# Causal attention with routed experts on one core: the two heads of a pair on the two 64-row halves of TensorE for maxima and scores

## The chip, the cores and the metric

One core of a Trainium2 chip runs the program. The metric is the device time of one execution in microseconds (us); lower is better. Engines are called as in the profile: PE is TensorE's matmul, PEld its weight load, DVE is VectorE, ACT is ScalarE, POOL is GpSimd, SP is SyncE.

## The reference

A causal attention layer over one sequence of 2048 tokens of width 256, then a layer of 16 routed experts (two a token) and two shared ones, each with a residual and a layer norm. The change touches the attention alone:

```python
# x: (1, 2048, 256); 16 heads of 16; k and v come from a latent of 64
qf = jnp.concatenate([q_nope, q_rope], axis=-1)      # rotary on 12 of 16
kf = jnp.concatenate([k_nope, k_rope], axis=-1)
scores = jnp.einsum('bhqd,bhkd->bhqk', qf, kf) * scale
scores = jnp.where(causal, -jnp.inf, scores)
weights = jax.nn.softmax(scores, axis=-1)
out = jnp.einsum('bhqk,bhkd->bhqd', weights, v)
x = _layernorm(x + out)
x = _layernorm(x + experts(x))
```

## The kernel before, in words

**Work and its units.** The queries are cut into four chunks of 512 tokens (`CH`), the 16 heads into groups of four (`GH`). A unit is one group of one chunk: 16 units, four a chunk. A step is one unit and one block of 128 keys: a unit of chunk c has 4(c + 1) steps, in all 160. `aux_at`, `max_at` are lists that say what else each step does.

**Numbers of full precision from fast matmuls.** q and k are each split into a high and a low part in a reduced format (`F32R`), and the three products hi x hi, hi x lo, lo x hi (`PARTS`) are made in one matmul: the 16 dimensions of a head are stacked three times, 48 rows (`SPLIT`). `k_stack` holds two heads of a pair below one another, 96 rows (`STACK`), plus two rows of ones. `q_stack` holds for each head its 48 rows, with zeros in the rows of the pair's other head, plus two rows with the negated maxima in two parts. So one matmul of 96 rows makes one head's products, and one of 98 rows (`ROWS`) the same with the row's maximum taken off.

**Maxima first.** For each query and head the maximum over its keys is found before the scores. `max_bank` (line 637) fills one bank of PSUM, 128 queries by up to 512 keys, with four matmuls and a mask's matmul (line 642) for the four diagonal blocks of a head, with one or two matmuls for the rest of a head's own chunk (`SHARED_BANKS`: 128 + 384 keys, 256 keys), and with one of 512 keys for each earlier chunk. `max_ps` has three banks (`MAX_BANKS`); bank n waits on `max_done` until the reduction of bank n - 3 is done. DVE reduces each bank (`reduce_bank`, lines 761 and 767). `max_at` spreads the banks over the steps, 5.44, 4.48, 3.88 and 3.90 a step by chunk (`BANKS_A_STEP`), and has a unit's last bank at least three steps ahead of its first score (`MAX_AHEAD`). Units of chunk c have 12 + 16c banks. When a unit's banks are reduced, DVE folds them (line 778), the job `("maxima", u)` has PE transpose them (line 614), DVE negates and splits them into `m_rows` (lines 801, 802), and ACT issues two transfers of `m_rows` into the last two rows of `q_stack` (`store_maxima`, line 496).

**A step.** On PE (`score_head`, `values`, and the loop at the end of its block): four times a quarter of the step's banks and one score matmul, 128 keys by up to 512 queries (line 675; fewer queries on the diagonal, so that the last four steps of a unit have 512, 384, 256 and 128); auxiliary jobs after the second and the fourth; at the end the values of the step before, `values(s - 1)`, four heads with 17 output columns each at PSUM partitions 0, 32, 64, 96, in two passes each (line 695). Scores have three banks (`SCORE_BANKS`) and each waits on `exp_done` for the exponential three before it. In the last unit, where no maxima are left, the scores use the banks of both, six. ACT makes the exponentials (line 543), one a head, and its share of the auxiliary jobs after the second and fourth. POOL masks `probs` on the diagonal (line 450) and rotates and splits q and k of later chunks.

**Auxiliary jobs**: per chunk one latent, eight rotary and two value projections (`projection`), per unit the maxima's transpose and the output's (`out`), 62 of them after the prologue. The split q and k are stored to DRAM by SP and loaded back into `k_stack` and `q_stack` (`store_piece`, `load_q`, line 324).

**Prologue.** Chunk 0 is projected, the zeros of `q_stack` are set by POOL and DVE, the ones of `k_stack` by POOL, which copies them to the other chunks by DMA; unit 0's maxima are made and stored, then the first score runs.

The order of the work is that of the lists, the same on each engine; nothing is reordered at run time.

## Time and profile before

| | |
|---|---|
| time, median of 3 runs | 870.14 us (864.45 to 874.48) |
| the profiled execution | 869.14 us |
| its span | 867.4 us |
| PE busy | 758.3 us (87%) |
| PEld busy | 487.5 us (56%) |
| DVE busy | 571.0 us (66%) |
| ACT busy | 409.5 us (47%) |
| POOL busy | 243.7 us (28%) |
| line 637, maxima | 832 matmuls, 257.8 us |
| line 675, scores | 609 matmuls, 234.1 us (and 31 more into `max_ps`) |
| line 695, values | 1280 matmuls, 151.9 us, mean of one 547 ns |
| line 767 and 761, reductions | 640, 353.1 us |
| line 543, exponentials | 291.1 us; one of 512 columns 603 ns |
| line 496, copies of maxima | 32 transfers, 8.0 KB each, 1.9 us to landing |

Busy time of PE counts matmuls whose ends are modelled, and neighbours overlap in it; the distance between two starts says more. The attention ends at about 590 us of the span, the rest is the experts' half. The granted clock is a share of 2.4 GHz: 1.0 is 2.4 and 0.5 is 1.2 GHz.

### The profile page before, as it was taken

Reading aid. Unit: us, or ns where it says so; the run is one execution under the profiler, and the core shown is the slowest. Engines: PE = TensorE matmul, PEld = TensorE weight load, DVE = VectorE, ACT = ScalarE, POOL = GpSimd, SP = SyncE. Lnnn points to the kernel's source line nnn. Section 1 sums busy time; section 2 is a strip of 40 time slices with the busy share of each in tenths; the row PEclk is TensorE's granted clock in tenths of the full one; section 3 lists DMA queues with packets and bytes.
Section 4 is the critical chain, followed back from the end, with each engine's and each line's share of the span. In section 5 each row is a group of like instructions: output and inputs, shape, how many; then the busy total and the mean of one; then the engine's idle time right before and its main releaser. Section 6 shows DMA issues by size and latency. Waiting matters only on the chain. (4 is left out here: it accounts for less than half of the span.)

```text
span 867.4 us, 14346 instructions
## 1 busy us (share of the span) xinstructions
PE 758.3 (87%) x4309; PEld 487.5 (56%) x4310; DVE 571.0 (66%) x1414; ACT 409.5 (47%) x891; POOL 243.7 (28%) x327
## 2 busy tenths in 40 slices
PE   4679998999999999999999999992779999999930
PEld 3566565655645655566455555431569976666610
DVE  6755868778687877876778787202584456666646
ACT  3124464656555656666566666691412332222203
POOL 6326182341351043107100000102007513333323
PEclk9659999999999999999799999996798999999975
DMA  3754225140062006002400000003997313333245
GB/s 126 185 138 117 74 61 161 38 116 20 2 153 68 2 1 146 2 2 61 134 1 2 1 2 1 2 1 103 335 276 258 121 54 90 97 98 95 88 136 185
DMA packets 46668, 77.00 MB, mean 89 GB/s; under 512 B 5983, under 2 KB 27231, under 8 KB 45743
## 3 DMA queue, kind: packets, MB, share of 16 engines
q1 hardware_dynamic: 37455, 57.72, 24.9%
q0 software_dynamic: 5184, 14.72, 5.0%
q10 hardware_dynamic: 3968, 3.80, 1.3%
q8 instruction: 32, 0.52, 0.3%
q14 instruction: 29, 0.24, 0.1%
HBM read 42.40 MB, written 33.45 MB: 87 GB/s over the span
## 5 line engine op out<-in xcount | busy, mean ns | idle before, releaser
L543 ACT ACTIVATE probs<-scores 128x512 f32<-128x512 f32 (+3 forms) x609 | 291.1, 536 | 199.6 <-PE scores L675 182.2
L767 DVE TENSOR_REDUCE mx<-max_ps 128x1 f32<-128x512 f32 (+3 forms) x576 | 308.8, 594 | 79.3 <-PE max_ps L637 78.5
L637 PE MATMUL max_ps<-k_stack,q_stack 96*128 96x512 f32 (+3 forms) x832 | 257.8, 370 | 13.4 <-DVE mx L767 5.7
L675 PE MATMUL scores<-q_stack,k_stack 98*128 98x512 f32 (+3 forms) x609 | 234.1, 396 | 7.0 <-DMA q_stack<-m_rows 4.1
L637 PEld LDWEIGHTS max_ps<-k_stack,q_stack 96*128 96x128 f32 x832 | 150.8, 201 | 133.0 <-DVE mx L767 81.7
L695 PE MATMUL pv_ps<-probs,v_ones 128*17 128x512 f32 (+3 forms) x1280 | 151.9, 547 | 2.7 <-ACT probs L543 1.9
L675 PEld LDWEIGHTS scores<-q_stack,k_stack 98*128 98x128 f32 x609 | 117.7, 196 | 48.0 <-ACT probs L543 26.0
L450 POOL TENSOR_SCALAR_AFFINE_SELECT probs<-probs 128x512 f32<-128x512 f32 x64 | 40.6, 635 | 344.5 <-ACT probs L543 344.4
L1140 POOL DMA_INDIRECT token_y<-ys,dest x47 | 45.3, 964 | 100.0 <-DVE dest L1496 49.8
L761 DVE TENSOR_REDUCE mx<-max_ps 128x4 f32<-128x512 f32 x64 | 44.3, 692 | 35.5 <-PE max_ps L642 33.9
L1262 PE MATMUL gu_ps<-w_up_sb,xg_t 128*128 x188 | 67.3, 481 | 0.4 <-ACT xg_t L1199 0.3
L1179 ACT ACTIVATE silu<-gu_ps 128x176 f32<-128x176 f32 x79 | 24.9, 317 | 89.1 <-PE gu_ps L1262 44.9
L1442 DVE TENSOR_TENSOR hidden<-silu,gu_ps 128x176 f32<-128x176 f32 x79 | 26.6, 337 | 36.8 <-ACT silu L1179 35.7
L1290 PE MATMUL y_ps<-w_dn_sb,hidden_t 88*128 x188 | 48.5, 380 | 0.4 <-DVE ys L1502 0.4
L695 PEld LDWEIGHTS pv_ps<-probs,v_ones 128*17 128x17 f32 x1280 | 21.5, 96 | 46.9 <-ACT probs L543 35.1
L1130 POOL DMA_INDIRECT slot_x<-x_sb,slot x32 | 31.2, 974 | 47.5 <-DVE slot L1428 38.0
L1199 ACT ACTIVATE xg_t<-xt_ps 128x256 f32<-128x256 f32 x47 | 18.0, 383 | 49.8 <-PE xt_ps L1320 49.7
L1262 PEld LDWEIGHTS gu_ps<-w_up_sb,xg_t 128*128 128x128 f32 x188 | 31.9, 189 | 15.7 <-issue 2.2
L1489 DVE SCALAR_TENSOR_TENSOR part_w<-xg,expert_f 128x1 f32<-128x1 f32 x94 | 16.3, 215 | 36.1 <-DMA token_y<-ys,dest 35.8
L1272 PE MATMUL gu_ps<-shared_up,x_t 128*128 128x352 f32 x192 | 37.9, 335 | 0.0
L1281 PE MATMUL ht_ps<-ident,hidden 128*88 128x128 f32 x158 | 30.9, 278 | 7.2 <-DVE hidden L1442 7.0
L1290 PEld LDWEIGHTS y_ps<-w_dn_sb,hidden_t 88*128 88x128 f32 x188 | 31.9, 190 | 3.5 <-issue 1.0
(169 smaller groups left out, 765.1 us busy)
## 6 DMA issues: line engine op xcount, KB each, us to landing
kq_split<-kq_stage SPq DMA_DIRECT2D x96, 128.0 KB, 2.4
k_stack<-kq_split SPq DMA_DIRECT2D x8, 768.0 KB, 6.4
q_stack<-kq_split SPq DMA_DIRECT2D x32, 192.0 KB, 4.8
xg<-slot_x SPq DMA_DIRECT2D x47, 130.0 KB, 2.1
slot_x<-blank SPq DMA_DIRECT2D x11, 520.0 KB, 7.6
w_up_sb<-w_up SPq DMA_DIRECT2D x4, 1408.0 KB
w_dn_sb<-w_dn SPq DMA_DIRECT2D x4, 704.0 KB
x_raw<-xT SPq DMA_DIRECT2D x4, 512.0 KB, 6.1
```

Source lines behind the costliest of these rows:

```text
L450: nc.gpsimd.affine_select(out=v, in_=v, compare_op=ALU.is_ge, fill=0.0, base=0, pattern=[[0, GH], [1, P]], channel_multiplier=-1).then_inc ...
L543: nc.scalar.activation(probs[:, s % 2, h, off:CH], score_bank(n)[:, off:CH], ACT.Exp)\
L637: ins = nc.tensor.matmul(max_ps[:, n % MAX_BANKS, at:at + keys], q_stack[0:STACK, u % 4, h, tile * P:(tile + 1) * P], k_stack[0:STACK, pai ...
L675: nc.tensor.matmul(score_bank(n)[:, off:CH], k_stack[:, 2 * g + h // 2, b * P:(b + 1) * P], q_stack[:, u % 4, h, off:CH], start=True, stop ...
L695: last = nc.tensor.matmul(pv_ps[32 * h:32 * h + DH + 1, off:CH], v_ones[:, b, GH * g + h, :], probs[:, s % 2, h, off:CH], start=(b == 0), ...
L761: nc.vector.tensor_reduce(mx[:, u % 2, h * TPC:(h + 1) * TPC, c:c + 1], max_ps[:, n % MAX_BANKS].rearrange("p (i k) -> p i k", i=TPC), AX. ...
L767: last = nc.vector.tensor_reduce(mx[:, u % 2, h * TPC + tile, column:column + 1], max_ps[:, n % MAX_BANKS, at:at + keys], AX.X, ALU.max)
L1130: pool.indirect_dma_start(out=slot_x, out_offset=bass.IndirectOffsetOnAxis(ap=slot[:, k, i:i + 1], axis=0), in_=x1[:, i, :], in_offset=Non ...
L1140: pool.indirect_dma_start(out=token_y, out_offset=bass.IndirectOffsetOnAxis(ap=dest[:, r:r + 1], axis=0), in_=ys[:, r, :], in_offset=None) ...
L1262: last = nc.tensor.matmul(gu_ps[:, par, 0:2 * INTER], x_of(k), w_up[:, e, k, :], start=(k == 0), stop=(k == KT - 1))
L1272: last = nc.tensor.matmul(gu_ps[:, n % 2, 0:2 * INTER], x1_t[:, a, k, i * P:(i + 1) * P], shared_up[:, b, half, k, :], start=(m == 0), sto ...
L1290: last = nc.tensor.matmul(y_ps[:, bank, 0:E], hidden_t[:, par, k, :], w_dn[:, e, k, :], start=(k == 0), stop=(k == 1))
```

## The change

The stacks get 128 rows: the first head of a pair has its 48 rows and two more at 0 to 49, the second at 64 to 113, each in `k_stack` and in `q_stack`. A matmul of a head uses the 48 or 50 rows of its own half; the zeros are gone, and `q_stack` has two head places a unit for four. The two heads' matmuls stand next to one another, each with its own wait: `max_pair` fills the banks n and n + 1 in turn part by part, masks come last, and two scores follow one another. The banks' order in the lists alternates between the heads of a pair. PE's loop goes by halves of a step: half of the banks, two scores, auxiliary jobs. The maxima go to two places, so ACT issues four transfers a unit, of eight rows of `m_rows` each, and `mx_rows` orders the rows by half; SP loads `k_stack` in two transfers a piece. POOL writes ones to rows 32 to 63 and 96 to 127 of the first chunk and copies two rows of each half to the three others.

```diff
--- before.py
+++ after.py
@@ -32,8 +32,8 @@
 GH = 4
 UNITS_PER_CHUNK = HEADS // GH
 SPLIT = 3 * DH
-STACK = 2 * SPLIT
-ROWS = STACK + 2
+ROWS = SPLIT + 2
+HALF_ROWS = P // 2
 NEG = -3.0e38
 
 PARTS = ((0, 0), (0, 1), (1, 0))
...
@@ -67,8 +67,10 @@
 
 
         c = u // UNITS_PER_CHUNK
-        return [(u, h, i, kb) for h in range(GH) for i in range(TPC) for kb in range(c)] + \
-               [(u, h, n, c) for h in range(GH) for n in range(len(SHARED_BANKS) + 1)]
+        return [(u, 2 * pair + par, i, kb) for pair in range(GH // 2) for i in range(TPC) for kb in range(c)
+                for par in range(2)] + \
+               [(u, 2 * pair + par, n, c) for pair in range(GH // 2) for n in range(len(SHARED_BANKS) + 1)
+                for par in range(2)]
 
     def bank_parts(bank):
 
...
@@ -161,6 +163,12 @@
     def quarters(items, n=4):
         return [items[len(items) * k // n:len(items) * (k + 1) // n] for k in range(n)]
 
+    def half(par, rows=ROWS):
+        return slice(HALF_ROWS * par, HALF_ROWS * par + rows)
+
+    def mx_rows(h):
+        return ((h % 2) * (GH // 2) + h // 2) * TPC
+
 
     kq_dram = nc.dram_tensor("kq_split", (NCH, 4, 2, 3, DH * GH, CH), F32, kind="Internal").ap()
 
...
@@ -174,8 +182,8 @@
         def sem(name):
             return ctx.enter_context(nc.semaphore(name))
 
-        k_stack = sb("k_stack", [ROWS, HEADS // 2, S], F32R)
-        q_stack = sb("q_stack", [ROWS, 4, GH, CH], F32R)
+        k_stack = sb("k_stack", [P, HEADS // 2, S], F32R)
+        q_stack = sb("q_stack", [P, 4, GH // 2, CH], F32R)
         v_ones = sb("v_ones", [P, S // P, HEADS, DH + 1])
         probs = sb("probs", [P, 2, GH, CH])
         w_raw = sb("w_raw", [P, 2048])
...
@@ -321,8 +324,7 @@
                     sp.wait_ge(pe_scores, GH * first_step[u - 3])
                 for par in range(2):
                     src = kq_dram[c, 2 * m + 1, par].rearrange("copy (d j) n -> (copy d) j n", j=GH)
-                    sp.dma_start(q_stack[par * SPLIT:(par + 1) * SPLIT, u % 4, par::2, :].bitcast(F32),
-                                 src[:, j0 // 2:j0 // 2 + 2, :]).then_inc(q_stacked, 16)
+                    sp.dma_start(q_stack[half(par, SPLIT), u % 4].bitcast(F32), src[:, j0 // 2:j0 // 2 + 2, :]).then_inc(q_stacked, 16)
 
             def load_chunk(c):
 
...
@@ -348,10 +350,13 @@
                 if is_q:
 
                     sp.wait_ge(kq_stored[0], 16 * 6 * (piece // 2 + 1))
+                    if piece == 1:
+                        sp.wait_ge(ones_low, 2)
                     if piece > 1:
-                        sp.wait_ge(k_stacked, 16 * (piece // 2))
-                    sp.dma_start(k_stack[0:STACK, 4 * m:4 * m + 4, c * CH:(c + 1) * CH].bitcast(F32),
-                                 kq_dram[c, n - 1].rearrange("two copy (d j) n -> (two copy d) j n", j=GH)).then_inc(k_stacked, 16)
+                        sp.wait_ge(k_stacked, 32 * (piece // 2))
+                    for two in range(2):
+                        sp.dma_start(k_stack[half(two, SPLIT), 4 * m:4 * m + 4, c * CH:(c + 1) * CH].bitcast(F32),
+                                     kq_dram[c, n - 1, two].rearrange("copy (d j) n -> (copy d) j n", j=GH)).then_inc(k_stacked, 16)
                     sp.wait_ge(kq_stored[1], 16 * 6 * (piece // 2 + 1))
 
             load_chunk(1)
...
@@ -396,16 +401,20 @@
                 pool.dma_start(x_tok[:], t["x"][c * CH:(c + 1) * CH, :].rearrange("(i p) n -> p i n", p=P))\
                     .then_inc(tok_loaded, 16)
 
-            nc.gpsimd.memset(q_stack[0:STACK, 0:2].bitcast(F32), 0.0).then_inc(zeros_low, 1)
-            link(nc.gpsimd.memset(k_stack[STACK:ROWS, :, 0:CH].bitcast(F32), 1.0))
+            for par in range(2):
+                nc.gpsimd.memset(k_stack[HALF_ROWS * par + 32:HALF_ROWS * (par + 1), :, 0:CH].bitcast(F32), 1.0)\
+                  .then_inc(ones_low, 1)
+            pool.wait_ge(ones_low, 2)
             link(nc.gpsimd.memset(ident[:], 0.0))
             link(nc.gpsimd.affine_select(out=ident[:], in_=ident[:], compare_op=ALU.not_equal, fill=1.0, base=0,
                                          pattern=[[-1, P]], channel_multiplier=1))
             nc.gpsimd.tensor_copy(ident_b[:], ident[:]).then_inc(consts_ready, 1)
 
             for c in range(1, NCH):
-                pool.dma_start(k_stack[STACK:ROWS, :, c * CH:(c + 1) * CH].bitcast(F32),
-                               k_stack[STACK:ROWS, :, 0:CH].bitcast(F32)).then_inc(ones_ready, 16)
+                for par in range(2):
+                    ones = slice(HALF_ROWS * par + SPLIT, HALF_ROWS * par + ROWS)
+                    pool.dma_start(k_stack[ones, :, c * CH:(c + 1) * CH].bitcast(F32),
+                                   k_stack[ones, :, 0:CH].bitcast(F32)).then_inc(ones_ready, 16)
             link(nc.gpsimd.memset(mask_b[:], 0.0))
 
             nc.gpsimd.affine_select(out=mask_b[:], in_=mask_b[:], compare_op=ALU.is_ge, fill=NEG, base=0,
...
@@ -489,12 +498,15 @@
 
             def store_maxima(u):
 
-                wait_read(act, ("maxima", u))
+                act.wait_ge(dve_read, by_dve[("maxima", u)])
                 if u:
-                    act.wait_ge(m_stacked, 32 * u)
-                for part in range(2):
-                    act.dma_start(q_stack[STACK + part:STACK + part + 1, u % 4].rearrange("o h n -> o (h n)").bitcast(F32),
-                                  m_rows[:, u % 2, part, :].bitcast(F32)).then_inc(m_stacked, 16)
+                    act.wait_ge(m_stacked, 64 * u)
+                rows = GH * TPC // 2
+                for par in range(2):
+                    for part in range(2):
+                        at = HALF_ROWS * par + SPLIT + part
+                        act.dma_start(q_stack[at:at + 1, u % 4].rearrange("o h n -> o (h n)").bitcast(F32),
+                                     m_rows[rows * par:rows * par + rows, u % 2, part, :].bitcast(F32)).then_inc(m_stacked, 16)
 
             def read_aux(job):
                 kind, c, n = job
...
@@ -622,32 +634,36 @@
                 else:
                     projection(job)
 
-            def max_bank(bank):
+            def max_pair(bank):
+
                 u, h, i, kb = bank
                 c = u // UNITS_PER_CHUNK
                 n = max_no[bank]
                 pair = (u % UNITS_PER_CHUNK) * 2 + h // 2
-                if n > MAX_BANKS:
-
-                    pe.wait_ge(max_done, n - MAX_BANKS)
-                own = kb == c
-                masked = own and i == 0
+                masked = kb == c and i == 0
                 parts = bank_parts(bank)
                 for tile, k0, keys, at in parts:
-                    ins = nc.tensor.matmul(max_ps[:, n % MAX_BANKS, at:at + keys], q_stack[0:STACK, u % 4, h, tile * P:(tile + 1) * P],
-                                           k_stack[0:STACK, pair, kb * CH + k0:kb * CH + k0 + keys],
-                                           start=((tile, at) == (parts[0][0], parts[0][3])), stop=not masked,
-                                           skip_group_check=len(parts) > 1)
+                    first = at == parts[0][3]
+                    for par in range(2):
+                        if first and n + par > MAX_BANKS:
+
+                            pe.wait_ge(max_done, n + par - MAX_BANKS)
+                        ins = nc.tensor.matmul(max_ps[:, (n + par) % MAX_BANKS, at:at + keys],
+                                               q_stack[half(par, SPLIT), u % 4, h // 2, tile * P:(tile + 1) * P],
+                                               k_stack[half(par, SPLIT), pair, kb * CH + k0:kb * CH + k0 + keys],
+                                               start=first, stop=not masked, skip_group_check=len(parts) > 1)
+                        if at == parts[-1][3] and not masked:
+                            ins.then_inc(pe_max, 1)
                 if masked:
-                    ins = nc.tensor.matmul(max_ps[:, n % MAX_BANKS].rearrange("p (i k) -> p i k", i=TPC), ident_b[:],
-                                           mask_b[:].unsqueeze(1).to_broadcast([P, TPC, P]), start=False, stop=True,
-                                           skip_group_check=True)
-                ins.then_inc(pe_max, 1)
+                    for par in range(2):
+                        nc.tensor.matmul(max_ps[:, (n + par) % MAX_BANKS].rearrange("p (i k) -> p i k", i=TPC), ident_b[:],
+                                         mask_b[:].unsqueeze(1).to_broadcast([P, TPC, P]), start=False, stop=True,
+                                         skip_group_check=True).then_inc(pe_max, 1)
 
             def max_unit(u):
 
                 c, g = divmod(u, UNITS_PER_CHUNK)
-                pe.wait_ge(k_stacked, 16 * (2 * c + g // 2 + 1))
+                pe.wait_ge(k_stacked, 32 * (2 * c + g // 2 + 1))
                 pe.wait_ge(q_stacked, 16 * 2 * (u + 1))
 
             def score_head(s, h):
...
@@ -669,11 +685,11 @@
                     wait_read(pe, prologue[len(prologue) // 2 * 2 - 1])
                 if b == 0 and h == 0:
 
-                    pe.wait_ge(m_stacked, 32 * (u + 1))
+                    pe.wait_ge(m_stacked, 64 * (u + 1))
                     if c:
-                        pe.wait_ge(ones_ready, 16 * (NCH - 1))
-                nc.tensor.matmul(score_bank(n)[:, off:CH], k_stack[:, 2 * g + h // 2, b * P:(b + 1) * P],
-                                 q_stack[:, u % 4, h, off:CH], start=True, stop=True).then_inc(pe_scores, 1)
+                        pe.wait_ge(ones_ready, 32 * (NCH - 1))
+                nc.tensor.matmul(score_bank(n)[:, off:CH], k_stack[half(h % 2), 2 * g + h // 2, b * P:(b + 1) * P],
+                                 q_stack[half(h % 2), u % 4, h // 2, off:CH], start=True, stop=True).then_inc(pe_scores, 1)
 
             def values(s):
 
...
@@ -715,15 +732,15 @@
             before_scores()
             for s in range(END):
 
-                banks, jobs = quarters(max_at[s]), quarters(aux_at[s], 2)
-                for half in range(2):
-                    for h in (2 * half, 2 * half + 1):
-                        run_banks(banks[h])
-                        if s < NS:
-                            score_head(s, h)
-                    for job in jobs[half]:
+                banks, jobs = quarters(max_at[s], 2), quarters(aux_at[s], 2)
+                for pair in range(2):
+                    run_banks(banks[pair])
+                    if s < NS:
+                        score_head(s, 2 * pair)
+                        score_head(s, 2 * pair + 1)
+                    for job in jobs[pair]:
                         run_aux(job)
-                    if half and 1 <= s <= NS:
+                    if pair and 1 <= s <= NS:
                         values(s - 1)
 
         @block.vector
...
@@ -758,13 +774,13 @@
                     dve.wait_ge(mx_ready, u - 1)
                 dve.wait_ge(pe_max, n)
                 if kb == c and i == 0:
-                    nc.vector.tensor_reduce(mx[:, u % 2, h * TPC:(h + 1) * TPC, c:c + 1],
+                    nc.vector.tensor_reduce(mx[:, u % 2, mx_rows(h):mx_rows(h) + TPC, c:c + 1],
                                             max_ps[:, n % MAX_BANKS].rearrange("p (i k) -> p i k", i=TPC), AX.X, ALU.max)\
                       .then_inc(max_done, 1)
                     return
                 column = kb if kb < c else c + 1
                 for tile, _, keys, at in bank_parts(bank):
-                    last = nc.vector.tensor_reduce(mx[:, u % 2, h * TPC + tile, column:column + 1],
+                    last = nc.vector.tensor_reduce(mx[:, u % 2, mx_rows(h) + tile, column:column + 1],
                                                    max_ps[:, n % MAX_BANKS, at:at + keys], AX.X, ALU.max)
                 last.then_inc(max_done, 1)
 
...
```

## Rows read from the trace of the kernel before

**Rows 1.** Windows 66 to 553 us; us, busy (x) of PE, PEld, DVE, ACT, POOL; PEclk, DMA
```profile
66.00:113.00 47.00, 43.16 (x304) 29.52 (x304) 33.06 (x75) 24.07 (x57) 18.86 (x30) 0.99 0.32 81
113.00:246.00 133.00, 126.70 (x785) 78.62 (x784) 102.28 (x208) 74.25 (x160) 53.41 (x78) 0.99 0.28 71
246.00:407.00 161.00, 157.39 (x944) 92.54 (x946) 123.15 (x238) 100.93 (x208) 42.53 (x62) 0.99 0.20 50
407.00:553.00 146.00, 142.24 (x799) 77.21 (x802) 111.80 (x210) 90.94 (x187) 10.55 (x16) 0.96 0.10 25
```
**Rows 2.** Waits from 66 to 553 us: us in total, times, longest
```profile
DVE mx L767 <- PE max_ps L637: 76.9, 104, 2.7
...
DVE mx L761 <- PE max_ps L642: 22.0, 30, 3.8
```
**Rows 3.** Timeline of one full step: start us, us, engine, line, tiles, xcount
```profile
514.64 0.50 PE L637 MATMUL max_ps<-k_stack,q_stack 96*128 96x512 f32 x1
...
514.98 0.40 PE L675 MATMUL scores<-q_stack,k_stack 98*128 98x512 f32 x1
...
515.17 2.48 DVE L767 TENSOR_REDUCE mx<-max_ps 128x1 f32<-128x512 f32 x4 [0.40 <-PE max_ps L637]
...
515.41 2.06 ACT L543 ACTIVATE probs<-scores 128x512 f32<-128x512 f32 x4 [1.44 <-PE scores L675]
...
516.39 0.39 PE L675 MATMUL scores<-q_stack,k_stack 98*128 98x512 f32 x1
...
516.71 1.05 PE L695 MATMUL pv_ps<-probs,v_ones 128*17 128x512 f32 x8
...
517.69 0.50 PE L675 MATMUL scores<-q_stack,k_stack 98*128 98x512 f32 x1
```
**Rows 4.** Timeline, a reduction and the weight load that waits for it
```profile
85.85 0.69 DVE L761 TENSOR_REDUCE mx<-max_ps 128x4 f32<-128x512 f32 x1 [0.32 <-PE max_ps L642]
...
86.60 0.19 PEld L637 LDWEIGHTS max_ps<-k_stack,q_stack 96*128 96x128 f32 x1 [0.35 <-DVE mx L761]
```
**Rows 5.** Timeline, a diagonal bank's four matmuls and its mask's
```profile
302.00 0.56 PE L637 MATMUL max_ps<-k_stack,q_stack 96*128 96x128 f32 x4
...
302.40 0.39 PE L642 MATMUL max_ps<-mask_b,ident_b 128*128 128x512 bf16 x1
```
**Rows 6.** Timeline of a step in which ACT issues copies of maxima
```profile
349.48 1.05 PE L695 MATMUL pv_ps<-probs,v_ones 128*17 128x512 f32 x8
...
350.85 1.16 ACTq L496 DMA_DIRECT2D q_stack<-m_rows  x2
...
352.12 2.06 ACT L543 ACTIVATE probs<-scores 128x512 f32<-128x512 f32 x4 [1.98 <-PE scores L675]
...
352.76 0.50 PE L675 MATMUL scores<-q_stack,k_stack 98*128 98x512 f32 x1 [0.39 <-ACT probs L543]
...
353.19 1.05 PE L695 MATMUL pv_ps<-probs,v_ones 128*17 128x512 f32 x8
```
**Rows 7.** Source view of line 496: ns min/median/max; then us to landing
```profile
L496 ACTq DMA_DIRECT2D q_stack<-m_rows x32: 510/594/717, 48.5 to 551.6; - x32
...
DMA to landing us min/median/max: 1.8/1.9/5.6
```
**Rows 8.** Timeline between units 13 and 14: copies, and the next unit's first score
```profile
503.23 1.16 ACTq L496 DMA_DIRECT2D q_stack<-m_rows  x2
...
505.97 0.40 PE L675 MATMUL scores<-q_stack,k_stack 98*128 98x512 f32 x1
```
**Rows 9.** Timeline, the first score of the kernel
```profile
53.92 0.80 PE L675 MATMUL scores<-q_stack,k_stack 98*128 98x512 f32 x1 [3.20 <-DMA q_stack<-m_rows]
```
**Rows 10.** Timeline of the last unit, the first scores of two steps
```profile
575.95 0.73 PE L675 MATMUL max_ps<-q_stack,k_stack 98*128 98x512 f32 x2
...
578.06 0.50 PE L675 MATMUL scores<-q_stack,k_stack 98*128 98x512 f32 x1
```
**Rows 11.** Windows view, 416 to 432 us, columns as in rows 1
```profile
416.00:432.00 16.00, 13.88 (x49) 6.60 (x49) 11.09 (x26) 6.88 (x13) 2.62 (x3) 0.68 0.53 145
```

More of the change, by code:

```diff
@@ L455, in _ @@
             pool.wait_ge(w_ready, 3)
-            pool.wait_ge(ones_ready, 16 * (NCH - 1))
+            pool.wait_ge(ones_ready, 32 * (NCH - 1))
             load_tokens(0)
@@ L704, in run_banks @@
                         max_unit(bank[0])
-                    max_bank(bank)
+                    if bank[1] % 2 == 0:
+                        max_pair(bank)
             def before_scores():
@@ L743, in _ @@
             nc.vector.memset(v_ones[:, :, :, DH:DH + 1], 1.0).then_inc(dve_consts, 1)
-            nc.vector.memset(q_stack[0:STACK, 2:4].bitcast(F32), 0.0).then_inc(zeros_high, 1)
             dve.wait_ge(hi_ready, 1)
```

9 lines of the change are left out of this document (2 added, 7 removed).

## Prediction

> **What bounds the kernel now.** Read the stages first. From 66 to 553 us, where maxima, scores and values run together, PE is busy 43.16 of 47 us, 126.70 of 133, 157.39 of 161 and 142.24 of 146, and DVE 33.06, 102.28, 123.15 and 111.80: together 370.3 of 487 us, so DVE idles 117 us [rows 1]. Of that idle time 76.9 and 22.0 us end with a matmul that fills a bank of `max_ps` [rows 2]. That looks like a PE bound with 117 us to win. A single step tells how much of it this change can reach [rows 3]. One step with four banks and four full scores runs from the maxima matmul at 514.64 to the next step's first matmul at 517.69: 3.05 us. From the score at 514.98 to the one at 516.39 lie six matmuls of 512 columns, 0.235 us apart. The first one of a step costs 0.34 (514.64 to 514.98), the last score to the values 0.32 (516.39 to 516.71), and the eight passes of the values hold PE for 0.98 (to 517.69). PE: 0.34 + 6 x 0.235 + 0.32 + 0.98 = 3.05, with no gap. DVE takes its four banks in 2.48 us, (2.48 - 0.69) / 3 = 0.60 apart, so 2.4 of 3.05; ACT its four exponentials in 2.06, (2.06 - 0.60) / 3 = 0.49 apart, so 1.95.
>
> **A step of four full banks.** If both matmuls of a pair run side by side, each pair takes one pitch, and PE's own work is 0.34 + 3 x 0.235 - 0.235 (first pair in the 0.34, then score pair, maxima pair, score pair) = 0.34 + 0.235 + 0.235, then 0.32 + 0.98, in all 2.11 us. DVE's 2.4 would then bound it. But there are still three banks of `max_ps`, and a pair takes two. The fourth maxima matmul of a step waits until DVE has emptied the bank of the step's first (`n + par - MAX_BANKS`), and behind it on PE, in order, stand two scores and the values. The chain of a step is: first matmul to its reduction 0.53 (514.64 to 515.17) [rows 3], the reduction 0.69 and its release 0.06 (85.85 + 0.69 = 86.54, load at 86.60) [rows 4], then the fourth maxima matmul 0.24, the score pair to the values 0.32, the values 0.98 [rows 3]. Sum 2.82 us. Before, the fourth matmul came at 0.34 + 5 x 0.235 = 1.5 us, after the release at 1.28, and waited for nothing. So a step gains 3.05 - 2.82 = 0.23 us, not the 0.94 that PE sheds.
> Units 4 to 15 have 384 full banks (16 x 4, 32 x 4, 48 x 4). In chunks 2 and 3, at some 3.9 a step, they fill 80 steps, and of these a quarter have the narrow scores of a unit's end, where 4 x 0.60 of DVE is the step's length already. In chunk 1, at 4.48 banks, every fourth or fifth step now holds three pairs, whose sixth matmul waits for the third reduction: no gain. 60 steps x 0.23 = **14 us less**. Bounds: 60 x (3.05 - 2.40) = 39 us if only DVE's pace counted, and 60 x (3.05 - 2.82 - 0.235) = 0 if the second score of a pair takes its own pitch.
> In the last unit no bank is left to fill and PE alone sets 578.06 - 575.95 = 2.11 us a step [rows 10]; with score pairs PE needs 1.64 and ACT's 1.95 binds: 12 full steps x 0.16 = **2 us less** (bounds: 6 less, none).
>
> **The diagonal banks** (12 a unit). Four matmuls of 128 columns start 0.10 us apart (302.00 to 302.40), then the mask's matmul follows [rows 5]; a 128-column stream is shorter than a 512 one, so it is the weight load that paces them. Per head 0.4 + 0.24. The pair does eight of them and both masks before DVE gets the second bank, and the second head's first one waits for a bank that stops the first head's too. If loads into the two halves overlap, four pitches are saved in a pair, 0.4 us; if not, none, and DVE starves about 0.4 longer at each first bank. Following the waits through the three steps of a unit's diagonal gives 0.5 us less with overlapping loads and 1 us more without, a unit. The trace has no row of a weight load beside another for halves of rows. I take **0**, between 16 x -0.5 = -8 and 16 x 1 = +16.
>
> **ACT's copies.** `store_maxima` issues four transfers for two. Each costs ACT 594 ns (median of 32), 1.9 us to landing [rows 7]. A step in which two are issued: ACT is at it from 350.85 to 352.01, its exponential begins at 352.12, the last score waits until 352.76, and the values come at 353.19, 3.71 us after 349.48 [rows 6], against 3.05 in a plain step: the first 1.16 us cost 0.66, the rest was ACT's slack. Two more find none: 1.16 to 1.2 us on score, values and next maxima. In chunk 3 the landing counts: issue from 503.23 to 504.39, first score that needs it at 505.97 [rows 8]; with four the last is issued at 503.23 + 3 x 0.58 = 504.97 and lands at 506.87, 0.9 late. At the start the first score, at 53.92, waits for just this transfer [rows 9], and two more issues put it off 1.2 us: **1 us more**. For the other 15 units 1.0 each, in chunk 0 half of that, as its steps are longer: **14 us more** (bounds 2, if DVE's filled banks cover them, and 15 x 1.5 = 22).
>
> **Changes of the array's shape.** The values, 17 columns in four column groups, are flanked by 0.32 and 0.34 where plain neighbours are 0.235 apart [rows 3]: 0.1 for each change. Scores and values change as before. New ones stand around each projection, transpose and mask: 62 auxiliary jobs between score pair and values, one more each, 62 x 0.1 = **6 us more** (bounds 0, and 12). Masks are in the diagonal's term.
> The Trainium skill, TensorEngine Tiling (Array Packing), Key Properties, says that changing the tiling mode drains TensorE, though changing the tile does not; the two 0.1 us beside the values agree. By that rule the term stands as above, and without it the sum would be 6 us less.
>
> **The rest.** The two memsets of `q_stack`, the k loads in two parts, three more copies of ones on POOL and one more strip of ones lie in the first 30 us, beside projections that wait for other things; the prologue's reads of the two stacks carry the same bytes. SP's queue has one more issue a piece, off every chain here. Taken as 0 (bounds -1, +3). The experts' half is not touched and shifts as a whole.
>
> **Sum.** -14 - 2 + 0 + 1 + 14 + 6 = +5. The profiled execution took 869.1 (span 867.4); the median of the runs is 870.1. So 874 to 875: I take **875**. A measurement of this kernel tells about 1% from no change.
>
> **Rivals.**
> DVE's pace sets the steps. If waits spread so that the idle 117 us [rows 1, 2] shrink by 45, a bit over the 39 of the bound, with diagonals at -8 and copies at +8: 870 - 45 - 2 - 8 + 8 + 6 = 829; half of it gives 850. It ends faster. For it: ACT and PE both have slack to give. Against: three banks, and the fourth matmul ahead of scores and values. It decides for the better once a full step takes under 2.7 us.
> The halves don't run side by side (the change doesn't do what it says). Each pair then costs two pitches: the chain has one more, 2.82 + 0.24 = 3.06, the step gains nothing, the diagonals are at +16, copies +15, changes +6: 870 + 37 = 907. Against it, the eight passes of the values, in four column groups, let PE go on after 0.98 us; one by one at the pitch of 512 columns they would take 8 x 0.235 = 1.9 [rows 3], so parts of the array do run together. The Trainium skill, TensorE: Matmul & The Clock Gate, Measured speedup vs the span model, gives 3.07 times for four row tiles; no run here shows row tiles.
> Copies, diagonals and changes are dear, with pairs that work: -14 - 2 + 8 + 1 + 20 + 9 = +22, so 892. For it: ACT can't issue until DVE has the rows, and a blocked ACT stops score, values and maxima in turn.
> The clock. PE now idles 0.7 of 2.8 us in a step. From 416 to 432 us, with PE busy 13.88 of 16 us, the granted clock was 0.68 [rows 11], a mix of 2.4 and 1.2 GHz. Short waits of 0.5 us don't look like that; if a tenth of 480 us ran at 1.2 GHz, 48 us of it would lengthen by 0.3 or so, 15 us: 890.
>
> **Chances.** Forecast (866 to 884) 0.38, DVE's pace 0.28, dear ends 0.17, no overlap 0.10, clock 0.07. The likeliest case straddles the bound of 1% above 870.1, 878.8. Faster by over 1% (under 861.4): the DVE case and a little of mine, 0.32. Within 1%: 0.29. Slower: 0.39. The range runs from 842, a bit past half of the DVE case, to 902, short of the no-overlap case.
>
> **What would show it.** Two maxima matmuls that start within 0.02 us of each other in pairs, likewise scores. A full step of 2.8 us with the values' first pass 1.8 after the step's first matmul, and PE waiting for DVE before the step's fourth maxima matmul; that wait, 0.06 us after a reduction ends, should be the largest of PE's. DVE busy some 85% in full steps. ACTq with 64 issues of 0.58, and in the step behind each four a start of the values over 4.5 us after the one before. The last unit at 1.95 a step, paced by ACT. I would be wrong if full steps took 2.5 (DVE paces) or 3.05 (no overlap), or if the four issues lengthened their step by no more than the two do.

## The result, and the profile after

The changed kernel takes 960.66 us (median of 4, 945.92 to 970.9), the kernel before 869.6 in the same comparison: ratio 1.0943, 95% interval 1.0857 to 1.1029. The ratio rests on the two fast executions of the four (945.92 and 957.22 us), while the profiled one is a slow one, so its loss of 94.5 us below is somewhat over the 82 us of the ratio. Forecast were 875 us and at most 902. The profiled execution took 964.11 (span 962.4).

First the page of the changed kernel: busy time, the clock in 40 slices, and the groups that answer to the table of before.

```profile
PE 807.5 (84%) x4309; PEld 424.8 (44%) x4310; DVE 566.1 (59%) x1413; ACT 406.4 (42%) x891; POOL 246.0 (26%) x330
...
PEclk9756675786567679795989789898769999999975
...
L651 PE MATMUL max_ps<-k_stack,q_stack 48*128 48x512 f32 (+3 forms) x832 | 239.4, 475 | 42.8 <-DVE mx L783 34.1
...
L691 PE MATMUL scores<-q_stack,k_stack 50*128 50x512 f32 (+3 forms) x609 | 192.2, 478 | 17.7 <-ACT probs L555 13.8
L711 PE MATMUL pv_ps<-probs,v_ones 128*17 128x512 f32 (+3 forms) x1280 | 187.5, 666 | 6.9 <-ACT probs L555 4.5
```

The values (L711) have not been edited, and yet a pass lasts 666 ns for 547 before. PEclk says why: it has many digits of 5 to 8 in the attention, above all in its first two thirds, where the kernel before has nearly all 9:

```profile
PEclk9659999999999999999799999996798999999975
```

Windows cut at the values' first matmul, at the chunks' borders and at the last one give the table below (us, busy time and count of PE, PEld, DVE, ACT, POOL, then the granted clock, DMA and GB/s). The changed kernel, in all, by chunk (the last one without its last unit), and the rest after the attention:

```profile
68.40:684.40 616.00, 555.98 (x3020) 236.83 (x3020) 370.90 (x730) 318.78 (x675) 129.04 (x190) 0.78 0.18 41
68.40:145.70 77.30, 70.10 (x387) 35.77 (x390) 40.57 (x91) 30.48 (x75) 33.70 (x51) 0.70 0.30 68
145.70:305.40 159.70, 145.90 (x707) 66.13 (x708) 95.67 (x194) 66.38 (x143) 40.65 (x61) 0.68 0.23 52
305.40:495.40 190.00, 174.31 (x939) 74.56 (x938) 123.41 (x238) 99.53 (x207) 41.70 (x61) 0.79 0.19 43
495.40:653.30 157.90, 138.91 (x819) 53.16 (x819) 110.56 (x209) 95.27 (x194) 10.45 (x16) 0.88 0.10 23
...
684.40:962.40 278.00, 210.10 (x1113) 157.62 (x1113) 157.09 (x609) 71.50 (x190) 88.73 (x98) 0.88 0.49 151
```

The kernel before, cut in the same way (all, chunks 0 to 3, and the rest):

```profile
66.50:588.00 521.50, 502.93 (x3020) 291.32 (x3019) 370.96 (x730) 321.32 (x675) 128.03 (x189) 0.98 0.19 48
66.50:126.20 59.70, 54.85 (x387) 36.92 (x390) 40.29 (x90) 31.31 (x75) 30.05 (x48) 1.00 0.31 77
126.20:246.50 120.30, 115.02 (x707) 71.08 (x708) 95.55 (x194) 67.52 (x143) 42.13 (x61) 0.99 0.28 71
246.50:407.00 160.50, 156.89 (x942) 92.40 (x945) 122.65 (x237) 100.43 (x207) 42.13 (x61) 0.99 0.20 50
407.00:557.20 150.20, 146.42 (x819) 79.26 (x818) 111.80 (x210) 94.33 (x195) 11.18 (x17) 0.96 0.09 24
...
588.00:867.40 279.40, 212.95 (x1113) 160.06 (x1113) 157.84 (x609) 71.61 (x190) 88.51 (x98) 0.87 0.49 150
```

The rest, 279.4 and 278.0, is the same. All of the loss is in the attention: 521.5 to 616.0, 94.5 us. DVE and ACT do the same work there. As the clock is granted at one of two levels, a mean of 0.78 puts 2 x (1 - 0.78) = 44% of 616 us at 1.2 GHz, 271 us; before it was 4% of 521.5, 21 us. "Cold" below is this product, from such a row of each run: the time at 1.2 GHz.

**At 2.4 GHz the step is what was forecast.** The timeline of a full step of the changed kernel, to be laid beside [rows 3]:

```profile
623.54 1.05 PE L711 MATMUL pv_ps<-probs,v_ones 128*17 128x512 f32 x8
...
624.53 0.50 PE L651 MATMUL max_ps<-k_stack,q_stack 48*128 48x512 f32 x2
...
624.86 0.40 PE L691 MATMUL scores<-q_stack,k_stack 50*128 50x512 f32 x2
...
625.06 2.48 DVE L783 TENSOR_REDUCE mx<-max_ps 128x1 f32<-128x512 f32 x4 [0.45 <-PE max_ps L651]
625.10 0.39 PE L651 MATMUL max_ps<-k_stack,q_stack 48*128 48x512 f32 x1
...
625.80 0.50 PE L651 MATMUL max_ps<-k_stack,q_stack 48*128 48x512 f32 x1 [0.32 <-DVE mx L783]
...
625.81 0.73 PE L691 MATMUL scores<-q_stack,k_stack 50*128 50x512 f32 x2
...
626.47 1.05 PE L711 MATMUL pv_ps<-probs,v_ones 128*17 128x512 f32 x8
```

Two maxima matmuls merge into one row of 0.50, and the scores start 0.33 later: the pair takes one place. The third goes at 625.10, the fourth waits for DVE until 625.80, 1.27 after the step's first; the forecast had 1.28. From values to values 2.93, for 3.05 before and 2.82 forecast: the values come 0.66 after the fourth maxima matmul, not 0.56. The first score of the last pair runs beside that matmul, on the other half; the second, on the same half, starts 0.34 after it (the row of two scores ends at 626.54, and one lasts 0.40), where the forecast had 0.24. The last unit: 1.96 a step, 1.95 forecast.

```profile
667.57 1.05 PE L711 MATMUL pv_ps<-probs,v_ones 128*17 128x512 f32 x8 [0.24 <-ACT probs L555]
...
669.53 1.05 PE L711 MATMUL pv_ps<-probs,v_ones 128*17 128x512 f32 x8 [0.24 <-ACT probs L555]
```

**At 1.2 GHz it isn't.** The next timeline is of a second execution of the same kernel (the control among the experiments). There a full step lies wholly at 1.2 GHz. It lasts 4.56, and eight passes of the values 1.91 for 1.05. The windows row of that step has the clock:

```profile
512.02 1.91 PE L711 MATMUL pv_ps<-probs,v_ones 128*17 128x512 f32 x8
...
516.58 1.91 PE L711 MATMUL pv_ps<-probs,v_ones 128*17 128x512 f32 x8
```

```profile
512.02:516.58 4.56, 4.56 (x18) 1.55 (x17) 2.23 (x5) 2.08 (x5) 0.00 (x0) 0.50 0.00 0
```

**The copies** open the longest regular pause. Timeline behind unit 14's maxima:

```profile
593.29 0.84 PE L711 MATMUL pv_ps<-probs,v_ones 128*17 128x384 f32 x8
...
594.02 2.78 ACTq L508 DMA_DIRECT2D q_stack<-m_rows  x4
...
596.90 0.98 ACT L555 ACTIVATE probs<-scores 128x128 f32<-128x128 f32 x4 [3.33 <-DMA q_stack<-m_rows]
597.24 0.34 PE L691 MATMUL scores<-q_stack,k_stack 50*128 50x128 f32 x1 [1.39 <-ACT probs L555]
597.50 1.05 PE L711 MATMUL pv_ps<-probs,v_ones 128*17 128x256 f32 x8
```

ACT issues for 2.78 us (1.16 before, [rows 6]); its next exponential is at 596.90, PE's last score waits 1.39 for it, and the values come 4.21 after the values before. The next step is cold: 3.71 us.

### The profile page after: what moved, and what is told of

Its sections match the earlier page's. It is cut to its first block and busy times, and to the rows that moved or that the text cites. A ratio compares the mean times of both kernels' runs of the same rounds, so it can differ in the third digit from the quotient of the medians.

```text
span 962.4 us, 14388 instructions
## 1 busy us (share of the span) xinstructions
PE 807.5 (84%) x4309; PEld 424.8 (44%) x4310; DVE 566.1 (59%) x1413; ACT 406.4 (42%) x891; POOL 246.0 (26%) x330
## 5 line engine op out<-in xcount | busy, mean ns | idle before, releaser
L783 DVE TENSOR_REDUCE mx<-max_ps 128x1 f32<-128x512 f32 (+2 forms) x576 | 307.6, 595 | 141.6 <-PE max_ps L651 140.8
L651 PE MATMUL max_ps<-k_stack,q_stack 48*128 48x512 f32 (+3 forms) x832 | 239.4, 475 | 42.8 <-DVE mx L783 34.1
L651 PEld LDWEIGHTS max_ps<-k_stack,q_stack 48*128 48x128 f32 x832 | 119.7, 234 | 245.5 <-DVE mx L783 143.8
L691 PE MATMUL scores<-q_stack,k_stack 50*128 50x512 f32 (+3 forms) x609 | 192.2, 478 | 17.7 <-ACT probs L555 13.8
L711 PE MATMUL pv_ps<-probs,v_ones 128*17 128x512 f32 (+3 forms) x1280 | 187.5, 666 | 6.9 <-ACT probs L555 4.5
L691 PEld LDWEIGHTS scores<-q_stack,k_stack 50*128 50x128 f32 x609 | 94.8, 230 | 67.5 <-ACT probs L555 42.2
L777 DVE TENSOR_REDUCE mx<-max_ps 128x4 f32<-128x512 f32 x64 | 41.5, 688 | 53.0 <-PE max_ps L659 53.0
L711 PEld LDWEIGHTS pv_ps<-probs,v_ones 128*17 128x17 f32 x1280 | 22.6, 101 | 54.7 <-ACT probs L555 36.8
L831 DVE RECIPROCAL recip<-aux_ps 128x16 f32<-128x16 f32 x16 | 4.1, 257 | 51.6 <-PE aux_ps L632 51.5
```

Source lines behind the costliest of these rows:

```text
L651: ins = nc.tensor.matmul(max_ps[:, (n + par) % MAX_BANKS, at:at + keys], q_stack[half(par, SPLIT), u % 4, h // 2, tile * P:(tile + 1) * P] ...
L691: nc.tensor.matmul(score_bank(n)[:, off:CH], k_stack[half(h % 2), 2 * g + h // 2, b * P:(b + 1) * P], q_stack[half(h % 2), u % 4, h // 2, ...
L711: last = nc.tensor.matmul(pv_ps[32 * h:32 * h + DH + 1, off:CH], v_ones[:, b, GH * g + h, :], probs[:, s % 2, h, off:CH], start=(b == 0), ...
L777: nc.vector.tensor_reduce(mx[:, u % 2, mx_rows(h):mx_rows(h) + TPC, c:c + 1], max_ps[:, n % MAX_BANKS].rearrange("p (i k) -> p i k", i=TPC ...
L783: last = nc.vector.tensor_reduce(mx[:, u % 2, mx_rows(h) + tile, column:column + 1], max_ps[:, n % MAX_BANKS, at:at + keys], AX.X, ALU.max)
```

## The experiments

All times of the attention are from the first values to the last, in the run's own trace. Each comes from one profiled execution, and executions of one kernel in one call differ by up to 25 us (945.92 to 970.9 above), so a few us between two traces decide nothing. The experts' half takes about 278 or about 313 us, the same for all kernels of a call (the kernel before took 869 in one call and 902 in another), so runs of different calls are compared by the attention, and by ratios. Where an expectation gives a time of the whole kernel, it is meant for a kernel before of 869.6 us. Theory at first: PE's pauses let the clock fall (P). Rival: matmuls that use half of the rows hold it down (H).

**Two copies for four.** One transfer fills a row of both halves.

```diff
-                for par in range(2):
-                    for part in range(2):
-                        at = HALF_ROWS * par + SPLIT + part
-                        act.dma_start(q_stack[at:at + 1, u % 4]...
+                for part in range(2):
+                    at = SPLIT + part
+                    act.dma_start(q_stack[at:at + HALF_ROWS + 1:HALF_ROWS, u % 4]...
```

> The changed kernel, with the maxima of a unit copied by two transfers from ACT for four (each fills the maxima row of both halves). Theory P (pauses): PE's own waits, for a bank and behind ACT's copies, let the granted clock fall; 275 us of 66 to 686 are at 1.2 GHz after the change, 21 us before. Then the copies are one cause of several: 15 x 1.2 = 18 us directly and about as much again in clock, 915 to 935, cold time 180 to 240 us. Theory H (halves): matmuls on one half of the rows hold the clock down in any order: 16 to 18 us less, 940 to 945, cold time as it is. Theory C (copies are the main cause): 870 to 890 and under 60 us cold.

Attention 587.2, clock 0.80 (235 cold), 29 us less than the change. The kernel took 969.84 for 903.73, a ratio of 1.073 or 933 of 869.6. That lies within P's range in time and in cold time. H had expected less of a gain, and C falls: the copies are one cause, not the main one.

**The order of before, on halves.** `max_bank` for one bank at a time, `quarters(max_at[s])`, one score behind each.

> The changed kernel's halves and four copies, but on PE the order of the kernel before: one bank, one score, four times a step, each bank filled by itself with its own wait. Neighbours of unlike half can still overlap (score of head 0 with the bank of head 1). Theory P: with no pair that needs two banks at once PE pauses less, above all at the diagonal banks: 885 to 915, cold time 60 to 140 us. Theory H: the rows used are the same, so 935 to 960, cold time over 200 us.

621.4, clock 0.77 (286 cold), and 1004.05 for 903.73, or 966 of 869.6. Pairing and its waits are not the cause: P missed. H held on the clock, and the time is 6 us over its range.

**Scores twice**, the same matmul issued a second time.

> The changed kernel, with each score matmul issued twice into its own bank (the same values twice), 609 more matmuls that nothing needs. Theory P: they fill PE's waits, so the clock stays up; a full step at 2.4 GHz costs at most 0.2 more, the cold time falls under 150 us, and the kernel gets faster by doing more: 900 to 940. Theory H: a second matmul on a half changes nothing of the clock, and the work comes on top: 965 to 1000. If the clock had no part in the loss: slower too.

626.8, clock 0.87 (163 cold), and 1010.64 for 903.73, or 972 of 869.6. The cold time fell by 108 us, nearly as P had it, and the added matmuls ate the gain, so the time is H's. Both theories were half right.

**The kernel before with the coarse order** (`quarters(max_at[s], 2)`, then two scores).

> The kernel before (96 and 98 rows, zeros, two copies), with only PE's order changed: half of a step's banks, then two scores, twice a step. Theory P in the form that the coarse order alone makes the pauses: 890 to 920 and over 80 us cold. In the form that it takes the halves' shorter work to open the pauses: PE still has 3.05 us of work a step, the fourth bank's wait ends before its turn, 868 to 880 and under 40 us cold. Theory H: 868 to 880 as well.

538.2, clock 0.97 (32 cold): in this one trace the order costs 17 us of waits with full stacks, a little over what was expected, and next to none of the clock. Full steps take 3.16 for 3.05:

```profile
485.33 1.05 PE L695 MATMUL pv_ps<-probs,v_ones 128*17 128x512 f32 x8
...
488.50 1.05 PE L695 MATMUL pv_ps<-probs,v_ones 128*17 128x512 f32 x8
```

**The change again**, as a control.

> The changed kernel itself, beside the three that follow, since chips differ in the experts' half: its attention (from the first values to the last) took 616 us in its first profile, of it 273 at 1.2 GHz. All theories: 600 to 630 us again, 250 to 290 cold.

618.6, clock 0.77 (285 cold): as the first profile (616.0). The two traces also price a cold us. Eleven steps (values to values) lie wholly at 2.4 GHz in one of them and wholly at 1.2 in the other; they sum to 33.1 us at 2.4 and to 52.1 at 1.2, so 0.36 of a cold us is lost (a full step: 4.56 for 2.92). The same reckoning over the five traces in this order, the filled kernels below among them, has 50 steps, 163 and 242 us, and 0.33.

**The kernel before on 48 rows.**

```diff
-  ... q_stack[0:STACK, u % 4, h, ...], k_stack[0:STACK, pair, ...]
+  ... q_stack[0:SPLIT, u % 4, h, ...], k_stack[0:SPLIT, pair, ...]
-  ... k_stack[:, 2 * g + h // 2, ...], q_stack[:, u % 4, h, off:CH]
+  ... k_stack[0:SPLIT, 2 * g + h // 2, ...], q_stack[0:SPLIT, u % 4, h, off:CH]
```

> The kernel before, with rows 0 to 47 alone in each maxima and score matmul, for all heads (left out: the other head's rows and the maxima's rows; the odd heads then meet only zeros). Count, order and length of PE's matmuls stay, nothing runs side by side and PE has no more pauses than before. Theory H (rows used at a time hold the clock down): attention of the kernel before, 521 us, grows to 580 or more, cold time from 21 to over 150. Theory P (pauses): 515 to 530, cold under 40. Theory A (what counts is rows times time, so that the change, which halves it, and this kernel are alike): as H, cold near 270.

756.1. This run decides between P and H. Its windows, the whole attention and 167 us of it, and one step there:

```profile
68.90:825.00 756.10, 750.02 (x3020) 396.43 (x3020) 388.45 (x730) 342.19 (x675) 128.14 (x188) 0.64 0.13 33
552.50:719.80 167.30, 167.30 (x533) 83.37 (x533) 80.55 (x137) 68.00 (x123) 6.92 (x11) 0.50 0.02 7
```

```profile
657.64 1.91 PE L695 MATMUL pv_ps<-probs,v_ones 128*17 128x512 f32 x8
...
660.07 0.62 PE L675 MATMUL scores<-q_stack,k_stack 48*128 48x512 f32 x1
660.50 0.62 PE L637 MATMUL max_ps<-k_stack,q_stack 48*128 48x512 f32 x1
...
663.19 1.05 PE L695 MATMUL pv_ps<-probs,v_ones 128*17 128x512 f32 x4
```

PE is busy 167.30 of 167.3 us, matmul behind matmul, and stays at 1.2 GHz: starts are 0.43 apart for 0.235, the step is 663.19 - 657.64 = 5.55 us. The kernel before has the same instructions and the same order, with 96 and 98 rows at clock 0.98, though 48 of them hold zeros. No pause explains it. Cold are 2 x (1 - 0.64) x 756 = 544 us, twice the change's. Other stretches of this attention were at 2.4 GHz, and what lifts the clock there was not looked into. One thing besides the rows differs, for the odd heads now meet only zeros; the filled halves below leave the products as they are.

**The kernel before with half the columns**: PE has the changed kernel's 2.1 us of work, and all rows.

> The kernel before, with 96 and 98 rows as they are, but half of the columns in the full maxima matmuls and in the scores (left out: half of those products; reductions and exponentials read the whole banks as before). PE then has 2.1 us of work in a full step, as the changed kernel at 2.4 GHz, and so its pauses, but all rows. Theory P: cold over 150 of the attention, and it takes over 520 us. Theory A: the same, cold near 270. Theory H: cold under 60, and the attention shrinks to 460 to 500, at DVE's pace and its chain of waits (2.8 to 2.9 a full step).

517.4, clock 0.87 (135 cold). None of the three expectations has these numbers: P wanted over 150 cold, A near 270, H under 60. So less work in time costs clock too, but half as much as the change does. Full steps take 2.59, by the forecast's chain with streams shorter by 0.11: first matmul to reduction 0.42, 0.69, 0.06, then 0.23, 0.21, 0.98.

**Pairs and scores twice**, in the order 0, 1, 0, 1.

> The changed kernel, with each pair of full banks and each pair of scores issued twice in the order 0, 1, 0, 1, so that the repetition runs side by side too; 992 more matmuls that nothing needs. PE has 3.05 to 3.2 us of work in a full step, as before the change. Theory P and theory A: the clock holds as in the kernel before, cold under 80, attention 540 to 570, faster than with half the work. Theory H: only one half's or both halves' 100 rows stay active at once; if pairs count as 100 rows it is as A, if each counts as 50, cold stays over 200 and the attention is over 616.

637.7, clock 0.91 (115 cold). Missed on time: full steps took 3.61, for the repetitions stand in the chain behind the fourth maxima matmul. The cold time lies between the two expectations (under 80, over 200): 50-row pairs, twice as many, still got less of the clock than 96 rows.

**Filled halves.** The two rows of maxima move to 62 and 63 of a half; rows 48 to 61 are zeros in `q_stack` and ones in `k_stack`. Maxima matmuls use 62 rows, scores 64. With two copies:

```diff
-ROWS = SPLIT + 2
+FILLED = 62
+ROWS = FILLED + 2
-  q_stack[half(par, SPLIT), ...], k_stack[half(par, SPLIT), ...]     # maxima
+  q_stack[half(par, FILLED), ...], k_stack[half(par, FILLED), ...]
```

> The changed kernel with two copies of maxima a unit (as e1) and halves that are filled: maxima matmuls use 62 rows of a half and scores 64, rows 48 to 61 being zeros in q and ones in k, the maxima in rows 62 and 63. Same products, same order, same count and columns of matmuls as e1_two_copies; a pair has 124 or 128 rows at once for 96 or 100. Theory H (rows in use count, zeros too, as the kernel before had 48 rows of zeros in each matmul): cold time of the attention falls from 230 to under 130, the attention from 587 to 510 to 550. Theory P (pauses alone, the rows were a side effect of the 48-row kernel's zeros): nothing changes, 580 to 595 and 210 to 250 cold.

> g1_filled_pairs with four copies of maxima a unit from ACT, as in the change, at rows 62 and 63 of each half. It sizes the prediction's term of the copies, 14 us, where the clock mostly holds: 12 to 18 us over g1_filled_pairs by the term alone, 886 + 15 = 901, ratio 1.03. With pauses that bring the clock down as well: 20 to 35 more, ratio 1.035 to 1.055. If DVE's filled banks cover them: under 5.

> The filled halves and two copies, with PE's order of the kernel before (a bank, a score, four times a step; each bank by itself). Only neighbours of unlike half overlap, so PE has some 2.4 to 2.6 us of work a step and pauses less than with pairs. Theory H: cold under 100, attention 500 to 540. Theory P: as g3_fine_two, within 10 us.

> The same as g2_filled_fine with 48 and 50 rows: the fine order, two copies, halves not filled. Attention of the fine order with four copies 621 us and 292 cold. Theory H: two copies take 20 to 30 off, 590 to 600, cold over 200. Theory P: the same; the pair g2, g3 is what tells the theories apart.

Windows of the attention, in this order: filled pairs with two copies, the same with four, filled in the fine order, the fine order not filled.

```profile
69.70:608.20 538.50, 476.77 (x3021) 207.06 (x3021) 369.11 (x730) 318.41 (x675) 129.38 (x190) 0.93 0.21 47
```

```profile
70.70:660.90 590.20, 520.08 (x3020) 222.69 (x3020) 370.65 (x730) 319.06 (x675) 129.00 (x190) 0.84 0.18 43
```

```profile
71.10:610.00 538.90, 490.37 (x3020) 228.11 (x3019) 371.07 (x730) 317.68 (x675) 128.01 (x188) 0.92 0.20 46
```

```profile
69.00:656.40 587.40, 543.00 (x3022) 252.25 (x3023) 372.54 (x730) 320.82 (x675) 127.97 (x188) 0.81 0.18 42
```

More rows in the same matmuls give 49 us back, 587 to 538, in either order: rows filled with zeros pay. H had expected this within some us in all three runs with two copies, and P no change. The fine pair was run in one call, with the same products and order. Against the kernel before: filled pairs 1.0135 (1.006 to 1.021), filled fine order 1.0324 (1.0272 to 1.0377), fine order not filled 1.0747 (1.0696 to 1.0797), four copies filled 1.0883 (1.0813 to 1.0953). And the copies, forecast at 14, cost 52 us here (590.2 - 538.5), over every expectation: the clock goes from 0.93 to 0.84, and the step behind them takes 4.12 us in unit 13 for 2.56. First the rows with two copies, then with four:

```profile
477.25 0.84 PE L719 MATMUL pv_ps<-probs,v_ones 128*17 128x384 f32 x8
478.06 1.07 ACTq L514 DMA_DIRECT2D q_stack<-m_rows  x2
479.81 0.63 PE L719 MATMUL pv_ps<-probs,v_ones 128*17 128x256 f32 x8
```

```profile
522.50 0.84 PE L721 MATMUL pv_ps<-probs,v_ones 128*17 128x384 f32 x8
523.31 2.62 ACTq L516 DMA_DIRECT2D q_stack<-m_rows  x4
526.62 0.63 PE L721 MATMUL pv_ps<-probs,v_ones 128*17 128x256 f32 x8
```

In unit 12 the same two steps take 3.88 and 3.87: there the longer issue is hidden. Not filled, the copies cost 29.

| attention us (cold us) | four copies | two copies |
|---|---|---|
| 48 and 50 rows | 616.0 (271) | 587.2 (235) |
| 62 and 64 rows | 590.2 (189) | 538.5 (75) |

Either cure alone brings 26 to 29 us, both 77.

**Scores twice in chunks 0 and 1 alone**, on the filled kernels, for the loss left there.

> g2_filled_fine with the scores of chunks 0 and 1 issued twice, to give PE there the work that it had before the change. In g2 the attention lost 21 us in chunk 0 (52 us cold) and 4 in chunk 1 against the kernel before, gained 9 in chunk 3 and nothing in chunk 2. Theory H with pauses: cold of chunk 0 under 10, its time 60 to 66, chunk 1 at 120 to 124, the whole at 0.99 to 1.00 of the kernel before. If PE's added work binds there instead: chunks 0 and 1 as in g2, ratio 1.02 to 1.03.

> g1_filled_pairs with the scores of chunks 0 and 1 issued twice. In g1 chunk 0 took 74 us with 38 cold, chunk 1 129 with 20. Theory H with pauses: cold of the two under 20, together 190 to 196 us for 203, ratio 1.00 to 1.01. The diagonal banks wait in pairs whatever the clock is, so chunk 0 stays 5 us above the 60 of the kernel before.

With the fine order the ratio is 1.0297 (1.0226 to 1.0368), the same within the intervals as the 1.0324 without the repetition: no gain, and the added work binds, as the second half of the expectation had it. With pairs the attention took 536.7 for 538.5 at clock 0.96, but the ratio is 1.0347 (1.0283 to 1.041) for 1.0135: a miss, since by the timed executions the repetition costs 2%.

**Copies from SP.** The body of `store_maxima` moves to SP, ahead of `store_piece` in the same step.

> The kernel before with its two copies a unit issued by SP instead of ACT. If ACT's being held is what a copy costs (0.66 us in the step of rows 6), 15 x 0.66 = 10 us less: ratio 0.985 to 0.995. If SP's other work holds the copies up (it waits there for rotated pieces), the first scores of units 4, 8 and 12 come late and it is 1.00 to 1.01.

> g1_filled_pairs with its two copies issued by SP. With ACT never held, PE's pauses behind the scores go: 10 us less directly and less cold time than g1's 79; ratio 0.985 to 1.005 for g1's 1.0135.

> The change as it is (48 and 50 rows, four copies) with the copies issued by SP. Where e1 with two from ACT had 587 us of attention and the change 616: if ACT's being held is the cost, 570 to 587, ratio 1.045 to 1.07; if the landing of four transfers is, 600 to 616, ratio 1.08 to 1.095. The clock's fall by half-filled arrays stays in any case: cold over 180.

All three miss: 1.0445 (1.0402 to 1.0488), 1.0604 (1.0543 to 1.0664), 1.1146 (1.1072 to 1.1219). In the kernel before with SP's copies the timeline shows a unit's first score held for 10.52 us. SP stores and loads pieces, and issues the copies of maxima only at 203.62. The second of them lands at 210.25, 6.0 us after its issue, for 1.8 in the median of all 32:

```profile
197.70 3.65 SPq L346 DMA_DIRECT2D kq_split<-kq_stage  x6
...
203.62 1.18 SPq L363 DMA_DIRECT2D q_stack<-m_rows  x2
204.89 6.92 SPq L324 DMA_DIRECT2D q_stack<-kq_split  x4
...
210.34 0.76 PE L675 MATMUL scores<-q_stack,k_stack 98*128 98x512 f32 x1 [10.52 <-issue]
```

The attention of the change itself took 610.8 with SP's copies, within the 600 to 616 that stood for the landing as the cost, while its ratio is over both ranges. So whether ACT's being held or the landing costs more was not settled by moving the copies; SP brings waits of its own. A queue that is free when the maxima come was not tried. No version beat the kernel before.

## Why the prediction was wrong

**The step that failed** is the clock. The sum was made for 2.4 GHz throughout, and the rival "The clock" was put aside with "Short waits of 0.5 us don't look like that", a chance of 0.07 and 15 us. From 21 to 271 cold us are 250 more, where the rival had 48. The rival's price, 0.3 of a cold us, was about right: measured on the same steps it is 0.36 (the control). So 250 x 0.36 = 90 of the 94.5 us are the clock's, by this estimate. None of the forecast's signs of being wrong came (full steps of 2.5 or 3.05 us, four issues that cost no more than two), for none of them looked at the clock. The forecast looked at idle time alone. It didn't ask how many rows the matmuls keep in use, which is what the change halves. The 48-row run, with no idle time, and the filled halves, with the products unchanged, show that the rows count; the half-column run shows that the thinner work adds to it.

**What the forecast had right.** The pairs run side by side. The fourth maxima matmul's wait sets the full step (1.27 us, forecast 1.28), and the 0.94 that PE sheds shrink to 0.12 (3.05 to 2.93; forecast 0.23). The last unit goes at ACT's pace. PE's largest wait, that of its weight loads, is for DVE's reductions in the maxima (140.8 us in the waits view of the changed kernel, 81.7 before). Weight loads of the two halves overlap: in the diagonal eight matmuls take 0.59 us to the mask, not eight times 0.10.

```profile
367.04 0.66 PE L651 MATMUL max_ps<-k_stack,q_stack 48*128 48x128 f32 x8
367.63 0.60 PE L659 MATMUL max_ps<-mask_b,ident_b 128*128 128x512 bf16 x2
```

**Mis-sized terms.** The full step's gain was 0.12 for 0.23, so over the forecast's 60 steps 7 us for 14. The last score follows the fourth maxima matmul by 0.34, the pitch that a step's first matmul has in [rows 3], and not by 0.24. No change of shape stands between these two, so the 0.1 us over the plain pitch, which the forecast read as agreeing with the rule of a drain, is not shown to be the price of such a change, and no run measured the 6 us of that term. The start came 1.9 us later (66.5 to 68.4) for 1.

The copies' term of 14 us was about right by itself. Two more issues hold ACT 1.6 us longer (2.78 for 1.16), which costs 1.5 us in some units and nothing in others. Of the 52 us on the filled kernels, 114 more cold us x 0.36 = 41 are the clock's, of the 29 on the others 36 x 0.36 = 13: 11 to 16 us are left. What the forecast lacked is that such a pause brings the clock down. With the full step and the start as measured, the sum at 2.4 GHz is 5 + 7 + 1 = +13, and 94.5 - 90 = 4 are left beside the clock (12 at the lower price of 0.33). That the two are this close is partly luck: the diagonal's term and the changes of shape were not measured apart, and the coarse order alone cost 17 us on full stacks.

**The other rivals.** DVE's pace (0.28) fell: no full step got near 2.4. "No overlap" (0.10) fell: pairs merge in every timeline. "Dear ends" (0.17) had 20 us for the copies, which at 2.4 GHz cost 11 to 16; it names waits of ACT that are there, and not the cause of the loss.

## What to carry to other kernels

A PE bound that is cut by using half the array isn't worth its columns alone: look up in the profile whether the clock held at full rate before, and count how many rows the new matmuls keep in use, since rows filled with zeros were worth 49 us here. After cutting the bound engine's work, add the chain through the buffers that are left; three banks gave a step of 2.93 us where the engine had 2.1 of work. And an extra DMA issue on an engine in the chain costs its full time wherever the step has no slack, and what its pause does to the clock can be more: here 52 us for the 14 that were added up.

## What the runs showed of the hardware that had not been expected

A PE busy 167.30 of 167.3 us with 48-row matmuls was granted 0.50 of the clock, and the same stream with 96 and 98 rows, half of them zeros, 0.96 over chunk 3. The Trainium skill, TensorE: Matmul & The Clock Gate, Why this matters for your kernels, asks for TensorE to be kept busy and free of idle gaps; this stretch had no gap and stayed cold, so by the trace that is not enough. Two row halves ran beside one another: two maxima matmuls took the place of one (the scores start 0.33 behind both), and the loads of weights of the two halves overlapped (eight matmuls of 128 columns in 0.59 us). The experts' half, the same work in all kernels, took 278 us in some calls (clock 0.88, 151 GB/s) and 313 in others (clock 0.83, 134 GB/s); chip number 7 is on record with either, so that the chip is not shown to be the reason.
